# A recurrence of 1250 dependent steps: the repeat of a wrong guess moved into the guess's branch, and the branch moved behind half of the logits

## The reference

```python
def step(carry, x_t):
    h, c = carry
    sel_in = jnp.concatenate([h, c, x_t], axis=-1)
    logits = sel_in @ W_sel.T + b_sel
    onehot = jax.nn.one_hot(jnp.argmax(logits, axis=-1), Sx, dtype=x_t.dtype)
    g_all = einsum('bi,sgi->bsg', x_t, W_ih) + einsum('bh,sgh->bsg', h, W_hh) + b_ih + b_hh
    g = jnp.einsum('bsg,bs->bg', g_all, onehot)
    h2, c2 = _lstm_activate(g, c)     # sigmoid, tanh; h2 = sigmoid(o) * tanh(c2)
    return ((h2, c2), h2)

x = x + gnn(layernorm(x), ..., 10)
x = x + lstm(layernorm(x)[None], ...)[0]
```

## Time and profile before

| | |
|---|---|
| median of three runs | 6861.82 us |
| the profiled execution | 6865.91 us, of which span 6864.2 us |
| mean granted clock of TensorE | 0.955 of full speed |
| busy share | PE 89%, PEld 60%, DVE 53%, ACT 26%, POOL 25% |
| step loop (1216 steps with a unit, 34 without) | about 1440 to 6840 us |
| first block's projection | 1274 to 1436 us |

### The profile page before, as it was taken

One profiled execution on the slowest core, in us unless ns is written; L12 is line 12 of the kernel. 1 busy time (PEld: TensorE's weight loads), 2 busy tenths in 40 slices (PEclk: granted clock), 3 DMA queues, 4 the chain that ended last, 5 costly groups with the idle time before them and its releaser, 6 DMA issues.

```text
span 6864.2 us, 340774 instructions
## 1 busy us (share of the span) xinstructions
PE 6126.8 (89%) x126674; PEld 4106.7 (60%) x126675; DVE 3617.9 (53%) x19152; ACT 1804.5 (26%) x6561; POOL 1685.8 (25%) x4128
## 2 busy tenths in 40 slices
PE   6727999679999999999999999999999999999986
PEld 3423444566666666666666666666666666666664
DVE  5453111235555556555665555566556665565555
ACT  1001000412233233222332332233333333233321
POOL 5732111412222222222222222222222222222220
PEclk8758999579999999999999999999999999999999
DMA  3220000522222122222222222222222222222210
GB/s 94 1 77 0 0 0 0 177 70 60 60 61 61 57 61 62 58 60 61 64 63 61 62 61 61 60 62 64 61 61 63 64 63 61 60 63 61 61 52 27
DMA packets 715589, 389.97 MB, mean 57 GB/s; under 512 B 47835, under 2 KB 703579, under 8 KB 715296
## 3 DMA queue, kind: packets, MB, share of 16 engines
q1 hardware_dynamic: 684322, 369.66, 18.4%
q0 software_dynamic: 24192, 0.10, 1.1%
q10 hardware_dynamic: 7038, 19.69, 0.9%
HBM read 370.96 MB, written 18.38 MB: 57 GB/s over the span
## 4 chain that ended last, share of the span: by engine, by line
PE 70%; issue 6%; DVE 6%; DMA 0%; DVEq 0%; SPq 0%; POOL 0%; ACT 0%; POOLq 0%
PE ps L1007 33%; PE ps L1069 15%; PE ps L1016 8%; PE ps L1000 5%; PE ps L996 4%; DVE hsum L837 2%; PE ps L993 2%; PE ps L983 2%; DVE osum L845 1%; DVE acts L855 1%; DVE gates L842 1%; DVE osum L848 1%; DVE cprod L851 0%; PE ps L972 0%; DMA wring<-in_w_ih 0%
## 5 line engine op out<-in xcount | busy, mean ns | idle before, releaser
L1007 PE MATMUL ps<-WH,hparts 128*2 128x384 f16 x49760 | 2297.3, 326 | 194.4 <-issue 173.2
L837 DVE TRANSPOSE_TENSOR_REDUCE hsum<-ps 128x12 f32<-128x384 f32 x1250 | 728.8, 583 | 1784.5 <-PE ps L1007 1774.2
L1007 PEld LDWEIGHTS ps<-WH,hparts 128*2 128x2 f16 x49760 | 1042.4, 83 | 1046.7 <-issue 297.0
L1069 PE MATMUL ps<-xcur,wcur 128*128 128x64 f32 x9728 | 1342.8, 281 | 89.1 <-issue 15.1
L1069 PEld LDWEIGHTS ps<-xcur,wcur 128*128 128x128 f32 x9728 | 1179.3, 191 | 276.6 <-issue 213.6
L449 POOL COPY xT<-hfull 128x4 f32 x1250 | 239.5, 192 | 3721.7 <-DVE hfull L866 3721.7
L465 POOL COPY wcur<-wring 128x512 f32<-128x512 f32 x1216 | 743.4, 611 | 449.7 <-ACT gxb L593 447.8
L1016 PEld LDWEIGHTS ps<-WH,hparts 128*2 128x2 f16 x40000 | 596.7, 83 | 359.0 <-issue 316.6
L1016 PE MATMUL ps<-WH,hparts 128*2 128x128 f16 x40000 | 775.4, 219 | 8.6
L578 ACT ACTIVATE gx_now<-gxb 128x16 f32 x1250 | 269.7, 216 | 1832.6 <-DVE pick L831 1709.3
L963 PE MATMUL ps<-O,Adj 128*128 128x512 f16 x3000 | 650.3, 380 | 77.2 <-DVEq L743 77.2
(11 more groups left out here) (147 smaller groups left out, 5001.8 us busy)
## 6 DMA issues: line engine op xcount, KB each, us to landing
wring<-in_w_ih SPq DMA_DIRECT2D x1280, 256.0 KB, 2.9
gxb<-in_w_hh ACTq DMA_DIRECT2D x32, 512.0 KB, 4.0
adjacency<-Adj SPq DMA_DIRECT2D x2, 6400.5 KB, 24.7
Adj<-adjacency SPq DMA_DIRECT2D x10, 640.0 KB, 7.3
sim<-adjacency SPq DMA_DIRECT2D x10, 640.0 KB, 6.5
adjacency<-total,where_ POOLq DMA_INDIRECT x168
x_rows<-X SPq DMA_DIRECT2D x1, 2560.0 KB, 8.7
wring<-x_rows SPq DMA_DIRECT2D x10, 256.0 KB, 3.6
```

The source lines that it names most:

```text
L837: dve.tensor_reduce(hsum[:, :], gate_ps.rearrange("p (c q) -> p c q", q=32), AX.X, ALU.add, apply_transpose=True).then_inc(turned, 1)
L1007: last = nc.tensor.matmul(gate_ps[32 * j:32 * j + 2, :], hparts[:, k, :], WH[:, s * KC + k, part, j, 0:3 * P], start=(k == 0 and part == 0 ...
L1069: last = nc.tensor.matmul(unit_ps, wcur[:, k, :], xcur[:, k, :], start=(k == 0), stop=(k == KC - 1))
```

## The change

Two places change on TensorE, and one on SP.

The ring's buffers hold, in the first block's projection, one quarter k of the inputs for four units, in place of one unit with all four quarters. SP's transfers bring 128 rows of 2 KB that lie together. TensorE's loop runs over k outside and the four units inside, so that four accumulators grow side by side; the wait for its own result stands once behind the four units, and three of the four buffers are freed by the last product that reads them.

In the step, `logits` becomes `early_logits` (input and c), which stands in front of the guess tree, and `late_logits` (tanh), at the start of each leaf. A wrong guess is repeated in the leaf, by one or two branches over the three other sets; behind the tree, only the products of the fourth gate are left for the chosen set.

```diff
-                    for u in range(SUB):
-                        sp.wait_ge(wring_free, sp.snap(q * (G * SUB) + (g * SUB + u + 1)))
-                        load_unit(q, g, u)
+                    for k in range(KC):
+                        sp.wait_ge(wring_free, sp.snap(q * (G * KC) + (g * KC + k + 1)))
+                        sp.dma_start(wring[:, k, :, :].rearrange("p u n -> p (u n)"),
+                                     w_ih[:, bass.ds(q, 1), order[g], k * D:(k + 1) * D].rearrange("p a n -> p (a n)")
+                                     ).then_inc(wring_in[k], 16)
...
-                for u in range(SUB):
-                    pe.wait_ge(wring_in[u], pe.snap(q * 16 + 16))
-                    pe.sem_inc(pieces_seen, 1)
-                    pe.wait_ge(proj_out, pe.snap(q * SUB + (u + 1)))
-                    for k in range(KC):
-                        last = nc.tensor.matmul(ps[:, 4 + u, 0:TB], wring[:, u, k, :], xT[:, k, 0:TB], start=(k == 0), stop=(k == KC - 1))
-                    last.then_inc(proj_mm, 1)
-                    pe.wait_ge(proj_mm, pe.snap(q * SUB + (u + 1)))
-                    pe.sem_inc(wring_free, 1)
+                for k in range(KC):
+                    for u in range(SUB):
+                        if u == 0:
+                            pe.wait_ge(wring_in[k], pe.snap(q * 16 + 16))
+                            pe.sem_inc(pieces_seen, 1)
+                        if k == 0:
+                            pe.wait_ge(proj_out, pe.snap(q * SUB + (u + 1)))
+                        last = nc.tensor.matmul(ps[:, 4 + u, 0:TB], wring[:, k, u, :], xT[:, k, 0:TB], start=(k == 0), stop=(k == KC - 1))
+                        if k == KC - 1:
+                            last.then_inc(proj_mm, 1)
+                        elif u == SUB - 1:
+                            last.then_inc(wring_free, 1)
+                pe.wait_ge(proj_mm, pe.snap(q * SUB + SUB))
+                pe.sem_inc(wring_free, 1)
...
-            def logits(n):
+            def early_logits(n):
                 pe.wait_ge(lx_set, n)
                 nc.tensor.matmul(logit_ps, ones[:, 0:1], lx_now[:, :], start=True, stop=False)
                 pe.wait_ge(c_ready, n)
                 for k in range(SUB):
                     nc.tensor.matmul(logit_ps, acts[:, 3 * SUB + k:3 * SUB + k + 1], wselT[:, k, :], start=False, stop=False)
+
+            def late_logits(n):
                 pe.wait_ge(tanc_ready, n)
                 pe.wait_ge(owsel_ready, n)
...
                 def guessed(s):
-                    logits(n)
+                    late_logits(n)
                     pe.wait_ge(h_ready, n)
                     cell_products(s, guess_mm)
...
                     with pe.If_eq(chosen, S - s):
                         pe.sem_inc(settled, 1)
                         output_products(s)
-
-                def repeated(s):
-                    cell_products(s, settled)
-                    output_products(s)
-
+                    with pe.Else():
+                        one, two, three = [other for other in range(S - 1, -1, -1) if other != s]
+                        with pe.If_lt(chosen, S - two):
+                            cell_products(one, settled)
+                        with pe.Else():
+                            with pe.If_lt(chosen, S - three):
+                                cell_products(two, settled)
+                            with pe.Else():
+                                cell_products(three, settled)
+
+                early_logits(n)
                 of_set(guess, guessed)
                 with pe.If_ne(chosen, guess):
-                    of_set(chosen, repeated)
+                    of_set(chosen, output_products)
```

## The result

The changed kernel takes **7045.78 us** (median of 4 runs, 7035.03 to 7049.16), against 6863.39 us for the kernel before (6860.64 to 6865.94): slower, ratio 1.0262, 95% interval 1.0246 to 1.0278. The forecast was 6932 us, the range 6850 to 7010: the direction was right, the size was not, and the time lies 36 us above the range.

A forecast was written before the change was run, and what follows sets the result against it. The prediction took each step to be bound by the fixed VectorE and ScalarE chain or by the choice. Its terms, 85 - 20 - 20 + 25 = +70 us, gave 6932 us against the median of 6861.8, range 6850 to 7010.

The forecast's parts named there:

- What bounds the kernel: In each step, the fixed VectorE and ScalarE chain, 3.78 us a step, or the choice beside it; hsum waits for both.
- the knee at 0.47 us: In a step, late logits starting later than about 0.47 us after c cost their further lateness in full.
- Part 1, the tree behind c: Right guesses: branches behind c's logits put late logits 0.42, 0.56 or 0.70 us after c; +85 us.
- Part 2, the repeat in the leaf: Wrong guesses: fewer branches before the repeat, partly lost to the later pick; -20 us, bounds -160 and +30.
- The rival of the repeat that catches up: Wrong guesses: repeated products start as guessed ones end, so the 0.52 us gap goes; -160 us, total 6792; chance 0.09.
- Part 3, the projection: First block's projection: one TensorE stop left per group of four units; -20 us, bounds 0 and -21.
- The rival of the full clock: Projection: passes without gaps run at clock 1.00, 86 us in place of 162; total 6876 us; chance 0.12.
- Part 4, more code: Longer step loops: more first touches of code, most in the last loop; +25 us, bounds 0 and +60.
- the last loop alone, 34 steps, up to +140, 7070 us: Rival case: only the last loop's code is fetched again, its steps stalling about 4 us; within the refetch rival's chance 0.13.
- a refetch of everything: Rival: the larger loop no longer stays resident; one main-loop step in ten stalls 4 us, +490, 7420 us; chance 0.13.

The follow-up runs named there:

- e6: The kernel before with only the logits of input and c moved in front of the guess tree: 6999.75 us, ratio 1.0211.
- e8: The changed kernel with its last loop of 34 steps as in the kernel before: 6896.93 us.
- e5: The kernel before with the projection by chunks and, in the main loop alone, the repeat in the leaf, all logits staying in the leaf: 10479.25 us.
- e1: The changed kernel with 102 records that never run between the main loop and the last loop: 6964.21 us.
- e3: The changed kernel with 122 records that never run ahead of the main loop: 11062.82 us.
- e4: The kernel before with the projection by chunks alone: 6826.87 us, ratio 0.9949.
- e7: e5 with 206 records that never run ahead of the main loop: 6775.82 us, ratio 0.9871.

## Why the prediction was wrong

*What bounds the kernel*: right. The step is the chain of fixed length or the choice, with the knee at 0.47 us, as the step lengths under part 1 show.

*Part 1, the tree behind c*: right. Forecast were late logits 0.42, 0.56 and 0.70 us after c; measured 0.42, 0.55 and 0.68 (212, 459 and 236 of the right steps between the 21st and the last but one of the main loop, sorted by where the logits start). From one c to the next these steps take 3.77, 3.87 and 3.99 us; forecast were 3.78, 3.87 and 4.0. (From first product to first product they are 3.80, 3.89 and 3.93, since the products of the latest group start 0.85 us after c and not 0.77, which that count gives to the step before.) The mean right step went from 3.783 to 3.879, over 945 right steps 91 us, where the term was 85. e6 shows that it is the branches and not the code's size: 143 us lost (6999.75 - 6856.42) with a shorter loop.

*Part 2, the repeat in the leaf*: right. Over the 288 wrong steps of the same stretch, from the end of the pick to the first repeated product, the mean fell from 1.405 to 1.181 us, and with the late pick the wrong step went from 5.871 to 5.797: 0.074 x 305 = 23 us, where the term was 20. A repeat in the set that is tested first (picked at 3209.31) shows 0.29 us of "issue", where the repeat of the earlier trace rows had 0.52:

```profile
3208.54 1.48 PE L1016 MATMUL ps<-WH,hparts 128*2 128x384 f16 x32
3209.16 0.15 DVE L833 TENSOR_REDUCE pick<-lmark 1x1 int32<-1x4 f32 x1
3210.30 1.47 PE L1016 MATMUL ps<-WH,hparts 128*2 128x384 f16 x32 [0.29 <-issue]
```

The rival of the repeat that catches up did not come: a gap remained.

*Part 3, the projection*: right in kind, too small. It gained 33 us, not 20, and lies outside the stated bound of -21. The stops went as said, one of 0.94 us in a group, but I kept four times 1.97 us for the four units. Put behind each other they take 7.08 us: a pass is recorded at 0.42 us, but the passes start 0.21 apart, so that each unit's 1.97 held the run-out of its last pass, which now overlaps the next unit:

```profile
1349.68 7.08 PE L987 MATMUL ps<-xT,wring 128*128 128x64 f32 x32 [0.94 <-DVE gxb L801]
...
1357.71 7.08 PE L987 MATMUL ps<-xT,wring 128*128 128x64 f32 x32 [0.94 <-DVE gxb L801]
```

16 groups of 8.03 us are 128.5. The rival of the full clock fell: the stage stayed at 0.50 though PE was busy 84.33 of 96 us.

*Part 4, more code*: **this is the step that failed.** "I take +25 us for more first touches, most of it in the last loop; bounds 0 and +60." Measured are 4.6 us ahead of the main loop and 148.1 in the last loop, twice the upper bound and more, and not as first touches: the loop lay across eight blocks, and the same blocks were fetched about nine times over (74 fetches, eight blocks). The case stood among the rivals ("the last loop alone, 34 steps, up to +140, 7070 us"), with a chance of 0.13 shared with a refetch of everything. What spoke against it, no fetch in 5160 us, was a fact about the old loop of some 1,235 records. The new loop's length was at hand, and that it came near to some limit was not to be read from any row of before; that should have widened the range rather than been settled by "the new loop fits". With the last loop set to what e8 measured, the forecast's other terms give 85 - 20 - 20 = +45 us, and e8 stands 38 above the kernel before of its own comparison (6896.93 - 6858.89).

The Trainium skill (Runtime: NRT & Kernel Launch, "Instruction fetch mechanics") gives TensorE a first-in first-out store of 128 KiB, filled in blocks of 16 KiB: that is eight blocks. I read its 2048 instructions as a bound on a loop's length. The runs agree with eight blocks if one of them goes to the block fetched ahead, which no run tests by itself: loops across seven settled, loops across eight never did, and 1767 records did either, by place. The Trainium skill's window of two blocks is contradicted by every loop here that settled, as the changed kernel's main loop, which ran 5160 us across seven blocks without a fetch.

## What to carry to other kernels

Before a loop with branches on TensorE is made longer, count the blocks of 256 records that it lies across, every copy of it too (where a block begins has to be read from a stall, as in e5), and look at the queue of code fetches stage by stage. Where a loop is fetched again, moving it by code that never runs can bring back most of what making it shorter does: the last loop of 309.0 us took 226.6 (e1) and 176.4 (e3) at another place, and 161.5 with shorter code (e8). A branch costs nothing where the engine waits anyway (the two that put the late logits at 0.42 us, below the knee, left the step at 3.77), and its full price where the next instruction is the one that the chain waits for (here each jump put the late logits 0.13 us further back), so move work in front of a branch only if the work behind it is not the later of the two. A change in several parts should be timed in parts: here gains of 32 us (e4) and 51 (e4 to e7) stood beside losses of 143 (e6) and 149 (e8).

## What the runs showed of the hardware

A loop's place in the code, with not one instruction more run in a step, moved this kernel between 6776 and 10479 us (e7 and e5) and between 7046 and 11063 (the changed kernel and e3). A loop across seven blocks did not always settle at once: 8 fetches stand at the start of e7's main loop, 14 at that of the changed kernel's, 29 in the last loop of e1. Of the 33 branches over 1 us in the changed kernel's last loop, 29 took 3.0 to 6.8 us; the branches of the main loop, where no code was fetched, took at most 0.22 us. And where TensorE waits for code its granted clock is lower too (0.69 in the changed kernel's last loop, 0.75 in e3's main loop): from 6716 to 7020 us the median product of L1016 is recorded at 0.480 us, in the main loop at 0.326.
